# Statistics of x tiles 11 to 15 one down product later, x tiles 12 to 15 requested by ScalarE, down weight loads behind a prefix load, one output multiply ahead of the sums

## The reference, cut to what matters

```python
xn = layernorm(x)                                   # no scale, no shift
q, k, v, gate = xn @ Wq, xn @ Wk, xn @ Wv, sigmoid(xn @ Wg + bg)
S_t = decay * S_(t-1) + (k_t gate_t) (v_t gate_t)^T # 64 x 64, over 4096 tokens
s = (q_t S_t) @ Wo + bo                             # recurrent layer
h = silu(xn @ wg.T) * (xn @ wu.T)                   # 1024 -> 3072, int32 weights / 127
g = silu(h @ wd.T)                                  # 3072 -> 1024
out = x + s * g
```

## Time and profile before

| | |
|---|---|
| median of 3 runs | 526.73 us (526.25 to 526.79) |
| the profiled execution | 528.42 us |
| span of its slowest core (6), first to last instruction | 526.9 us |
| spans of the eight cores | 520.8 to 526.9 us |
| PE busy on core 6 | 504.5 us, 96% |
| VectorE, ScalarE, GpSimd busy | 360.0 (68%), 188.4 (36%), 121.8 (23%) |

### The profile page before, as it was taken

One profiled execution on the slowest core, in us unless ns is written; L12 is line 12 of the kernel. 1 busy time (PEld: TensorE's weight loads), 2 busy tenths in 40 slices (PEclk: granted clock), 3 DMA queues, 4 the chain that ended last, 5 costly groups with the idle time before them and its releaser, 6 DMA issues.

```text
span 526.9 us, 8803 instructions; the slowest of 8 cores (520.8 to 526.9 us)
## 1 busy us (share of the span) xinstructions
PE 504.5 (96%) x2722; PEld 239.1 (45%) x2722; DVE 360.0 (68%) x683; ACT 188.4 (36%) x296; POOL 121.8 (23%) x189
## 2 busy tenths in 40 slices
PE   4799989999999999998899999999999999999996
PEld 2455544445554444444355444444444444444442
DVE  5768667666678779886575667666666667967444
ACT  3524445544444321248311443333333333112111
POOL 3636312222327000335242521111111100000000
PEclk9999999999999999999899999999999999999999
DMA  7999999998999540386679874654564600041342
GB/s 212 223 114 158 162 167 154 138 156 133 147 166 202 85 153 29 88 251 187 195 182 202 204 129 77 99 82 70 74 93 70 102 1 0 1 161 60 121 139 80
DMA packets 37452, 66.77 MB, mean 127 GB/s; under 512 B 3295, under 2 KB 12639, under 8 KB 37408
## 3 DMA queue, kind: packets, MB, share of 16 engines
q0 software_dynamic: 18672, 36.19, 46.0%
q1 hardware_dynamic: 15504, 28.32, 17.1%
q10 hardware_dynamic: 3232, 1.72, 1.3%
HBM read 89.28 MB, written 8.39 MB: 185 GB/s over the span
## 4 chain that ended last, share of the span: by engine, by line
PE 81%; DMA 10%; DVE 4%; issue 2%; POOL 1%; ACT 1%; SPq 0%; DVEq 0%; POOLq 0%; ACTq 0%
PE bank L476 50%; PE bank L532 24%; DMA xr<-xpfm 3%; DMA xs<-xtm 3%; DMA wa<-wall 2%; DMA gu<-wgu 2%; PE bank L638 1%; PE bank L657 1%; PE bank L544 1%; DVE bst L862 1%; DVE bst L863 1%; PE bank L692 1%; PE bank L693 1%; PE bank L678 0%; DVE xs L851 0%
## 5 line engine op out<-in xcount | busy, mean ns | idle before, releaser
L476 PE MATMUL bank<-xs,S_w 128*128 128x512 f16 x552 | 139.8, 379 | 1.7 <-ACT bank L1185 1.7
L476 PE MATMUL bank<-xnT,gu 128*128 128x512 f16 x368 | 94.5, 379 | 0.0
L476 PEld LDWEIGHTS bank<-xs,S_w 128*128 128x128 f16 x552 | 52.0, 98 | 62.1 <-issue 1.8
L1226 POOL DMA_DIRECT2D gu<-wgu x48 | 26.1, 545 | 187.3 <-PE bank L476 175.6
L1059 DVE TENSOR_TENSOR bank<-bank,m 128x512 f32<-128x512 f32 x46 | 32.2, 699 | 50.3 <-PE bank L476 50.3
L476 PEld LDWEIGHTS bank<-xnT,gu 128*128 128x128 f16 x368 | 34.7, 98 | 40.0 <-issue 0.2
L744 DVE SCALAR_TENSOR_TENSOR hT<-bank,sg_all 128x512 f16<-128x512 f32 x69 | 47.0, 688 | 6.5 <-PE bank L476 5.4
L1067 DVE TENSOR_TENSOR m<-bank,m 128x512 f32<-128x512 f32 x46 | 31.8, 691 | 26.8 <-PE bank L476 26.6
L476 PE MATMUL bank<-xs,gu 128*128 128x512 f16 x184 | 47.3, 380 | 0.0
L476 PE MATMUL bank<-xnT,S_w 128*128 128x512 f16 x184 | 47.2, 379 | 0.0
L532 PE MATMUL bank<-wd,hT 128*128 128x512 f16 x192 | 44.1, 379 | 0.0
(11 more groups left out here) (158 smaller groups left out, 718.4 us busy)
## 6 DMA issues: line engine op xcount, KB each, us to landing
gu<-wgu POOLq DMA_DIRECT2D x96, 256.0 KB, 7.8
xr<-xtm SPq DMA_DIRECT2D x16, 512.0 KB, 4.5
out<-xr SPq DMA_DIRECT2D x32, 256.0 KB, 2.2
xs<-xtm SPq DMA_DIRECT2D x12, 512.0 KB, 5.4
wd<-wdt POOLq DMA_DIRECT2D x24, 256.0 KB, 10.5
xr<-xpfm POOLq DMA_DIRECT2D x8, 512.0 KB, 12.7
hT<-gu SPq DMA_DIRECT2D x5, 512.0 KB, 5.2
wd<-xtm SPq DMA_DIRECT2D x4, 512.0 KB, 16.1
```

The costliest lines, as they stand in the source:

```text
L476: mm = pe.matmul(out=out[:], lhsT=weight(d), rhs=moving(d), start=(start and d == 0), stop=(d == 3), skip_group_check=True)
L1226: g.dma_start(out=gu[idx % NGU][:, 0:1024], in_=wgu[idx % NHC][:, 0:1024]).then_inc(ld_gate[idx % NGU], 16)
```

## The change

The statistics of x tiles 11 to 15 move from behind products 10 to 14 of the first down stage to 11, 12, 13, 15 and 16, their norms, transpositions and copies with them (two or three places behind their statistics, as before). The loads of x tiles 12 to 15 are issued by ScalarE, at places 9, 10, 11 and 13, and no more by SyncE at 9 to 12. Down weight loads 2 and 3 leave the prefix stage, and all from 2 on get new windows: 2 to 11 in windows 8 to 29, 12 to 23 in windows 30 to 43. Prefix load 2, in window 7, so has 2 of them ahead and not 5. The differences TD (0, 1, n) move to windows 34, 34, 35, 37, 39, 44. In the second down stage the multiply and the sum `dfin` (4, 0) go ahead of `addM` 4 and the sums of group 5, while its store stays behind product (4, 7).

```diff
--- before.py
+++ after.py
@@ -59,18 +59,15 @@
             else:
                 out += sums(1, 2)
         elif m == 2:
-            out += [("wo", (P, 0)), ("dsilu", (P, 0))]
+            out += [("wo", (P, 0)), ("dsilu", (P, 0)), ("dfin", (P, 0))]
             if P != 4:
-                out.append(("dfin", (P, 0)))
                 behind = tail(0)
         elif m == 7:
             out += [("wo", (P, 1)), ("addM", P)]
             if p == 0:
                 out += sums(1, 2)
-            if P == 4:
-                out += [("dfin", (P, 0))] + tail(0)
             out += [("dsilu", (P, 1)), ("dfin", (P, 1))]
-            behind = tail(1)
+            behind = (tail(0) if P == 4 else []) + tail(1)
         elif m == 3:
             out += [("wo", (P, 2)), ("dsilu", (P, 2)), ("dfin", (P, 2))] + sums(3) + tail(2)
         else:
@@ -101,7 +98,7 @@
     order += [("gate", 2), ("plain", 2), ("up", 2), ("h", 1), ("TS_0", 1), ("h", 2), ("kvg", 4), ("kvg_ev", 4),
               ("px_load", 1)]
     order += [("gate", 3), ("plain", 3), ("up", 3), ("h", 3), ("TS_1", 1), ("kvg", 5), ("kvg_ev", 5),
-              ("wd_load", 0), ("wd_load", 1), ("decay_2", 0), ("wd_load", 2), ("wd_load", 3)]
+              ("wd_load", 0), ("wd_load", 1), ("decay_2", 0)]
 
     slots = [[] for _ in range(4 * NPAIR)]
     slots[4] = [("kvg", 6), ("kvg_ev", 6), ("cw", 0)]
@@ -124,7 +121,7 @@
     slots[42] += [("px_scale", 1)]
     slots[43] += [("S0", 0)]
     slots[44] += [("res_load", 0), ("res_load", 1)]
-    for n, pos in enumerate((32, 32, 34, 36, 38, 44)):
+    for n, pos in enumerate((34, 34, 35, 37, 39, 44)):
         slots[pos].append(("TD", (0, 1, n)))
     slots[45].append(("SD_early", (0, 1)))
     slots[46].append(("SD_early", (0, 2)))
@@ -135,8 +132,8 @@
     for pos in range(4, 4 * NPAIR):
         order.append(("win", pos))
         order += slots[pos]
-        order += [("wd_load", n) for n in range(4, 13) if 6 + (n - 4) * 8 // 3 == pos]
-        order += [("wd_load", n) for n in range(13, NHC) if 29 + (n - 13) * 5 // 4 == pos]
+        order += [("wd_load", n) for n in range(2, 12) if 8 + (n - 2) * 7 // 3 == pos]
+        order += [("wd_load", n) for n in range(12, NHC) if 30 + (n - 12) * 5 // 4 == pos]
     order += [("x_load", 8 + i) for i in range(NXS)]
 
     order += [("SD_late", (0, 1)), ("SD_late", (0, 2))] + [("TD", (0, 2, n)) for n in range(3)]
@@ -144,14 +141,15 @@
     hooks = {0: [("recur", 4)], 1: [("score", 5), ("mask", 5)], 3: [("recur", 5)], 4: [("score", 6), ("mask", 6)],
              6: [("recur", 6), ("score", 7), ("mask", 7)], 8: [("recur", 7)]}
     hook = lambda k: hooks.setdefault(k, [])
+    at = (7, 8, 9, 11, 12, 13, 15, 16)
+    norms = {at[j] + 2: [("norm", 8 + j)] for j in range(1, 8)}
     for j in range(8):
-        hook(7 + j).append(("stats", 8 + j))
-    norms = {9 + j: [("norm", 8 + j)] for j in range(1, 8)}
+        hook(at[j]).append(("stats", 8 + j))
     hook(8).append(("norm", 8))
     for j in range(8):
         if j < 4:
-            hook(9 + j).append(("x_load", 12 + j))
-        hook(10 + j).extend([("tr", 8 + j), ("ev", 8 + j)])
+            hook(at[j] + 2).append(("x_load", 12 + j))
+        hook(at[j] + 3).extend([("tr", 8 + j), ("ev", 8 + j)])
         hook(18 + j).extend([("kvg", 8 + j), ("kvg_ev", 8 + j)])
     hook(22).extend([("gu_pre", 24), ("gu_pre", 25)])
     hook(24).extend([("gu_pre", 26), ("gu_pre", 27), ("gu_pre", 28)])
@@ -1215,6 +1213,9 @@
                     s.activation(out=m5[i % 2][:], in_=D_D[:], func=AF.Copy).then_inc(act_dseed, 1)
                 elif stage == "dsilu":
                     dsilu(*i)
+                elif stage == "x_load" and i >= 12:
+                    s.wait_ge(act_norm, i - NXS + 1)
+                    s.dma_start(out=x_tile(i), in_=xtm[i * 128:(i + 1) * 128, :]).then_inc(x_landed(i)[0], 16)
                 elif stage == "tcopy_act":
                     s.wait_ge(pe_dprod, dprod(0, 4))
                     s.dma_start(out=bass.AP(hT, 0, [[NHC * NH, 128], [NH, 24], [1, 256]]),
@@ -1318,11 +1319,9 @@
         @block.sync
         def _(y):
             for stage, i in order:
-                if stage == "x_load":
-                    if 8 <= i < 12:
+                if stage == "x_load" and i < 12:
+                    if i >= 8:
                         y.wait_ge((pe_m5, pe_m6, pe_m7, pe_m4)[i - 8], 2 * (NPAIR - 1))
-                    elif i >= 12:
-                        y.wait_ge(act_norm, i - NXS + 1)
                     y.dma_start(out=x_tile(i), in_=xtm[i * 128:(i + 1) * 128, :]).then_inc(x_landed(i)[0], 16)
                 elif stage == "res_load":
                     if i == 0:
```

## The result

The changed kernel takes 524.18 us (median of 4; 523.61 to 524.51), the kernel before in the same comparison 526.76 (526.25 to 527.76): a ratio of 0.9948, 95% interval 0.9930 to 0.9965, so 2.6 us less. The forecast was 521.8 us, 519.6 to 524.4. The sign and the range held; the size did not, 4.9 us were forecast. Executions in which the cores of one die show a much lower granted clock, 7 of 68 of the kernel before beside the experiments, are left out throughout.

The account below looks back on a forecast made before the run. PE's products and waits on the slowest core were taken as the bound. Core 2's terms, 526.0 - 4.3 - 1.1 + 1.0 + 0.9 - 0.5, gave 522.0, 4.9 under 526.9; median 526.73 became 521.8 us, range 519.6 to 524.4.

Parts of the forecast that it names:

- A: About 76 us, PE waits for ScalarE's copy, prefix tile 2 being late; removal: -4.3 us core 2, -1.7 core 6.
- E: New wait at the product of 165.00 us, opening window 39, for VectorE's late addition: 0.9 us on every core.
- B: At 238.12 us an output product waits 0.72 us for a multiply behind a statistics block; claimed gone, -0.7.
- F: New waits in the first down stage at x tiles 11 and 12, 0.4 and 0.6 us, together 1.0.
- C: Later x tiles' transpositions wait 0.52 us at 246.49, 2.12 at 255.30 on core 6 plus 1.7 clock; claimed gone.
- D: At 461.85 us an output product waits 0.77 us for a multiply; the change was to gain 0.5.
- the signs: Expected in the profile: no copy waits, new wait 0.8 to 1.1 us, tile waits under 0.8, cores within 2.
- All waits go and nothing new comes: Rival for the whole kernel: the old waits vanish with no new ones, 519.6 us; chance 0.22.
- The prefix tile comes no sooner: Rival at about 76 us: prefix tile 2 stays late, core 2 keeps its wait, 526.1 us; chance 0.07.
- the chain becomes the bound: Rival in the first down stage: tiles 11 to 15 each 1.8 us late, 9 us in all, 529.8 us; chance 0.06.

Follow-up runs that it names:

- the issuer undone: Changed kernel with SyncE issuing the loads of x tiles 12 to 15 again, all else as changed: 523.21 us, ratio 0.9934.
- the issuer alone: Kernel before with only the loads of x tiles 12 to 15 issued by ScalarE: 524.62 us, ratio 0.9972.
- the second profile: Changed kernel run and profiled again with no edit: 523.88 us, ratio 0.9956.
- the down weight order alone: Kernel before with only the down weight loads and differences placed as in the changed kernel: 525.60 us, ratio 0.9978.

## Why the prediction was right, and where it was wrong

**Down weight loads (A).** Right in mechanism and size. Three pieces of 1.6 us were costed at 4.8; the medians of the tile's landing fell by 5.1 (15.5 to 10.4), and the step between, with four pieces ahead, lies where the pieces put it. On core 6 the row "58.42 16.34 DMA xr<-xpfm" became 9.4 us, while VectorE's load in the stretch hardly changed. The windows view of core 6 after, columns as in the earlier trace rows:

```profile
58.00:75.00 17.00, 17.00 (x107) 8.26 (x106) 12.06 (x30) 9.11 (x15) 6.74 (x11) 1.00 1.04 141
240.00:262.00 22.00, 21.07 (x135) 10.97 (x133) 15.30 (x33) 13.36 (x16) 10.56 (x14) 1.00 0.70 204
```

VectorE is busy 12.06 us, 12.24 before, and the tile lands 7 us sooner; the queue set its time. The rule of the Trainium skill (SBUF — State Buffer, "SBUF: two separate sides"), by which GpSimd can't write descriptors while VectorE runs a two-port operation, was not what decided here. That VectorE's work in this stretch is of that kind was assumed in the prediction, and no view shows it.

**Differences of down weights (E).** Right. 0.9 was taken, 0.86 came, 0.60 of it from the L794 of window 37 and 0.26 from the power that comes late; the text had 0.6 for the first, and 1.0 for the late power less what hides.

**Statistics (B, F).** The sum for a core without C was -1.2 + 1.0 = -0.2 and measured -0.33. But two of its terms were less sure than they looked. B was put down to the block of statistics ahead of the multiply. Moving the block does remove B (the issuer undone), but so does the issuer alone with the block where it was, so the block was one of two things that could clear it. F was taken as 1.0, waits of 0.4 and 0.6 at tiles 11 and 12; they are 0.23 and 0.53. The 0.53 was there before: it stood at the same product (15), ahead of tile 13 (0.52). The prediction took C's 0.52 off in its 1.2 and put it back in F, so that these cancel.

**x tiles from ScalarE (C).** Gone, with its clock (0.92, now 1.00 in the second row above). On core 7 tile 15 is issued as forecast:

```profile
242.50 0.33 ACTq L1218 DMA_DIRECT2D xs<-xtm  x1
```

and lands 4.5 us later, at 247.0. Counted from the first window it was issued at 199.1 us, by SyncE before at 202.6 (core 6). The stage is 0.33 us longer with ScalarE as issuer, where the prediction had 0; one issue that is not covered would make just that, but the place of the loss has no issue in it. The Trainium skill (DMA: Bandwidth & Descriptors, "Issuing engines are not separate DMA queues") says that another issuer saves only issue time; the trace agrees, with 4.1 to 7.7 us from issue to landing for tiles 12 to 15 on ScalarE (cores 0, 3, 6 of the changed kernel, two profiles) and 3.7 to 7.1 on SyncE (the same cores before). What was won is the moment of issue, 3.5 us earlier.

**The output product (D).** Right: -0.5, measured -0.56.

**The sum: the step that failed.** Core by core it was good: 522.0 and 521.6 us for cores 2 and 6, measured 520.4 and 521.1. Of core 2's 1.6 us, 0.9 is an earlier first window (40.93 for 41.83) and 0.6 the wait for `qtk`, which it had before and has no more: luck, both. It failed in its last sentence: "4.9 off gives 523.5 for it and 521.8 us for the median of 526.73". The 1.69 us between the profiled execution and the median were carried along as if they were part of any execution. They were part of what the change removes: the profiled execution had A with its clock on two cores and tile 15 with its clock on a third, and its slowest span, 526.9, was 2.0 over the median one, 524.9. A change that takes away the chance waits brings each execution near the same floor, so its gain in the median is the median's excess over that floor, not the profiled one's. By the runs: slowest span 524.9 before, 522.3 to 522.6 after, 2.3 to 2.6 less. The sum of the prediction itself gave 522.0 for the slowest core; with 1.5 us around it that is 523.5, and no second subtraction was due. The rest, to 524.2, is the second thing it lacked: with A and C gone, the slowest core is the one with the latest start (core 7 in the profiled execution) or one with the wait for `qtk` (core 1 in the second profile). The first window began at 40.2 to 43.5 us over all profiles, and the prediction took each core's start as fixed; core 7's went from 41.26 to 43.45.

The band around the forecast, 520.3 to 523.6, does not come out of the terms either: the bounds of E and F alone give 519.9 to 523.1, and the upper end needs D at nothing as well. Of the signs, the cores lie 2.6 us apart and not within 2, and the new wait is 0.69 us and not 0.8 to 1.1; the others came (no waits behind ScalarE's copy, each wait at a tile under 0.8, no 5 us after 45 us up to the last store with a clock under 0.99).

**What the parts are worth.** From the ratios: the issuer alone 1.5 us, the down weight order alone 1.2, statistics, issuer and output order together 2.4, all 2.3 to 2.7. Each has an interval of 0.6 to 1.0 us either side. The parts with the down weight order (1.2) and without it (2.4) add up to more than the whole, as they would if the slowest core is slow by one wait or by the other, but the intervals leave room for a plain sum. The down weight order on top of the rest is worth nothing that can be measured: E costs every core 0.86, and A costs some cores 0.6 to 1.9. With load 4 alone moved and the differences left in place there is no E, and A is 0.23 us on one core.

**The rivals.** "All waits go and nothing new comes" was wrong in E. "The prefix tile comes no sooner" and "the chain becomes the bound" are refuted by the 9.4 us and by waits of at most 0.53 at a tile.

## What to carry to other kernels

Where cores that run one program differ, read the best core first: it shows what a change does to every core, and the others show chance waits. Look whether neighbouring cores draw them together. Price a chance wait against the median execution's slowest core, never against that of one profiled execution, and ask what makes the slowest core when it is gone. Here a load that was wanted soon came 1.65 to 1.8 us later for each piece of 262 kB ahead of it in a full queue; moving the one piece that was just ahead was enough, and moving more brought a new wait elsewhere.

## What was not expected of the hardware

- TensorE's granted clock fell behind waits of 2.41, 2.46, 2.12, 2.07 and once 1.84 us, and not behind others of 1.87, 1.69, 1.66 and 1.65: over the 5 us behind the wait it was 0.67 to 0.68 in the first group and 1.00 in the second. Each fall cost 1.6 to 1.7 us more. So of two waits near 1.85 us one cost itself and the other nearly twice itself.
- An issue of a 512 kB x tile on ScalarE takes 0.33 us, half of the 0.69 of its other DMA; on SyncE most take 0.38.
- Of two neighbouring cores mostly one is slow: both above 523.5 us in 4 of 244 pairs, exactly one in 149.
- GpSimd's power took 2.92 us in place of 3.26 with no L796 beside it, 0.34 less, as the prediction took it (0.3).
